# Experts' products from fp16 parts of both operands, the first layer's weights read in place

## The reference

```python
normed = _layernorm(hidden_states, rn_g, rn_b)
logits = (jnp.einsum('bld,ed->ble', normed, router_w) + router_b).astype(jnp.float32)
top_w, top_idx = jax.lax.top_k(logits, K)
...
for e in range(E):
    h = _layernorm(hidden_states, ln_g[e], ln_b[e])
    h = jax.nn.gelu(jnp.einsum('bld,di->bli', h, w1[e]) + b1[e], approximate=False)
    h = jnp.einsum('bli,id->bld', h, w2[e]) + b2[e]
    out = out + combine[..., e:e + 1] * h
```

## Time and profile before

| | us |
|---|---|
| median of 3 runs (lowest to highest) | 3234.09 (3232.27 to 3234.14) |
| span of the profiled execution | 3232.2 |
| attention, window 240 to 2460: PE busy | 2179.22 of 2220 |
| the same: DVE busy | 2213.41 of 2220 |
| experts, window 2700 to 3190: PE busy | 490.00 of 490 |
| experts, same: DVE, ACT, POOL busy | 194.25, 151.98, 247.68 |

### The profile page before, as it was taken

The page is one execution under the profiler, slowest core; times in us unless marked ns, Lnnn a source line. Parts: engine busy times, 40 slices in busy tenths (PEclk is TensorE's granted clock), DMA queues, the critical chain, the costliest instruction groups (busy, mean ns, idle before and its releaser), DMA issues. The chain is left out here.

```text
span 3232.2 us, 72457 instructions
## 1 busy us (share of the span) xinstructions
PE 3089.3 (96%) x29281; PEld 1389.4 (43%) x29282; DVE 2735.8 (85%) x2902; ACT 2502.6 (77%) x4689; POOL 453.2 (14%) x654
## 2 busy tenths in 40 slices
PE   8999999999999999999999999999999969999995
PEld 4333333333333333333333333333332658999995
DVE  3599999999999999999999999999998683433443
ACT  3269999999999999999999999999999552333333
POOL 2000000000000000000000000000000464555554
PEclk9989999999999999999999999999999979999997
DMA  6520101111020101011010101021002561222224
GB/s 159 124 45 15 35 21 30 30 34 28 15 35 24 28 15 35 29 30 28 28 28 18 34 21 28 15 51 28 15 9 83 206 227 34 38 38 36 36 37 124
DMA packets 101213, 152.92 MB, mean 47 GB/s; under 512 B 21592, under 2 KB 64464, under 8 KB 99248
## 3 DMA queue, kind: packets, MB, share of 16 engines
q1 hardware_dynamic: 85008, 130.03, 16.2%
q0 software_dynamic: 15904, 18.66, 3.6%
HBM read 88.35 MB, written 60.29 MB: 46 GB/s over the span
## 5 line engine op out<-in xcount | busy, mean ns | idle before, releaser
L1005 DVE TENSOR_REDUCE half_max<-scores 128x2 f32<-128x1024 f32 x2016 | 2297.4, 1219 | 10.5 <-PE scores L759 4.8
L930 ACT ACTIVATE probs<-bank 128x512 f32<-128x512 f32 x4012 | 2142.3, 595 | 142.5 <-PE bank L772 45.5
L831 PE MATMUL bank<-probs,V 128*32 128x256 f32 x16384 | 1309.6, 391 | 44.2 <-ACT probs L930 42.4
L759 PE MATMUL scores<-K,Q 48*128 48x512 f16 x4032 | 793.9, 388 | 3.0 <-SPq L542 2.2
L772 PE MATMUL bank<-Q,K 50*128 50x512 f16 x4012 | 789.7, 380 | 0.0
L831 PEld LDWEIGHTS bank<-probs,V 128*32 128x32 f32 x16384 | 322.5, 108 | 583.2 <-issue 517.7
L759 PEld LDWEIGHTS scores<-K,Q 48*128 48x128 f16 x4032 | 194.2, 93 | 834.6 <-DVE half_max L1005 532.2
L772 PEld LDWEIGHTS bank<-Q,K 50*128 50x128 f16 x4012 | 371.2, 94 | 183.0 <-ACT probs L930 4.2
L660 POOL TENSOR_SCALAR max_parts<-row_max 128x16 f16<-128x16 f32 x64 | 16.2, 253 | 2066.3 <-DVE row_max L1011 2066.3
L1604 ACT ACTIVATE h<-u 128x1024 f32<-128x1024 f32 x71 | 75.0, 1057 | 260.8 <-DVE u L1648 260.8
L1565 PE MATMUL pre<-xgT,w 128*128 128x128 f32 x2272 | 265.3, 275 | 2.3 <-ACT xgT L1598 2.3
(11 more groups left out here) (195 smaller groups left out, 1204.8 us busy)
## 6 DMA issues: line engine op xcount, KB each, us to landing
attended<-att SPq DMA_DIRECT2D x64, 256.0 KB, 2.5
W<-in_L_ffn_w_dram SPq DMA_DIRECT2D x16, 1024.0 KB, 6.4
Q<-q_parts SPq DMA_DIRECT2D x96, 128.0 KB, 6.6
K<-k_parts SPq DMA_DIRECT2D x96, 128.0 KB, 6.9
values<-attended SPq DMA_DIRECT2D x6, 2048.0 KB, 9.2
q_parts<-parts SPq DMA_DIRECT2D x64, 128.0 KB, 2.4
k_parts<-parts SPq DMA_DIRECT2D x64, 128.0 KB, 2.4
xT<-in_x_cols_dram SPq DMA_DIRECT2D x8, 512.0 KB, 4.9
```

Source lines behind the costliest of these rows:

```text
L759: mm = nc.tensor.matmul(scores[:, b, h, :], Q[p][r, c, up, t * P:(t + 1) * P], K[p][r, up, kc * TC:(kc + 1) * TC], start=True, stop=True)
L831: mm = nc.tensor.matmul(banks[att_bank[s // KB]][32 * u:32 * u + 32, q], V[wp][:, wk, u // 2, :], probs[:, 4 * s % RING + u, q], start=(wk ...
L930: nc.scalar.activation(probs[:, i % RING, :], banks[tile_bank[i]][:], ACT.Exp, scale=SCALE).then_inc(exp_done, 1)
L1005: nc.vector.tensor_reduce(half_max[lc % 2][:, :, up, t, kc], scores[:, b], AX.X, ALU.max).then_inc(max_done[b], 1)
```

## The change

Every float32 product of the experts' layers becomes three fp16 products. A float32 operand a is written as high + low, where high is a in fp16, and low is the rest in fp16; high x high, high x low and low x high are added up in PSUM. Weights are first multiplied by 2 to the 10th and activations by 2 to the 3rd, and the biases' additions take the factor out again (`UNLIFT`).

- The weights are split in the attention, by POOL (`split_w`): three instructions of 128 x 1024 for each of 4 units per pair, 32 units in all. SP loads each unit (`load_w`, 512 KB) and stores the two parts of w1 to DRAM (`store_w1`, `w1d`, 16 stores of 512 KB). The parts of w2 stay in `W2`, whose size in bytes is as before. The routing stage loads `W1` from `w1d`, as many bytes as before. POOL also clears the semaphores of the first stage that are no longer used.
- `take_w1` goes. `times_w1` reads `W1` in place: PE's sequencer loads the owner a second time per tile, and the weight operand has a register offset. 16 float32 matmuls become 48 fp16 matmuls of 128 columns.
- The second layer's 8 float32 matmuls become 24 fp16 matmuls of 256 columns, 16 with the high part of `h`, and then, behind a wait of their own, 8 with the low part.
- DVE splits the scaled rows (`high_x`, `low_x`, 128 x 256 each) and makes the low part of h (`low_h`, 128 x 1024). ACT makes its high part (`hs`). The order of the steps on ACT and DVE is changed with it.

```diff
+LIFT_W = 10
+LIFT_X = 3
...
+    w1d = nc.dram_tensor("w1_parts", (E, P, 2, KD, I), F16, kind="Internal").ap()
...
-        W2 = top.enter_context(nc.sbuf_tensor("W2", [P, E, IC, D], F32))
+        W2 = top.enter_context(nc.sbuf_tensor("W2", [P, E, 2, IC, D], F16))
...
-        W1 = top.enter_context(nc.sbuf_tensor("W1", [P, E, KD, I], F32))
+        W1 = top.enter_context(nc.sbuf_tensor("W1", [P, E, 2, KD, I], F16))
...
@@ -581,6 +590,23 @@
                 sp.dma_start(x1d[0:NT * P].rearrange("(p n j) d -> n p j d", p=P, n=QUADS)[q], x1[q % 2]
                              ).then_inc(x1_stored[q % 2], 16)
 
+            UNITS_W = 2 * KD
+
+            def load_w(it, m):
+                if it * UNITS_W + m >= 2:
+                    sp.wait_ge(w_split, it * UNITS_W + m - 1)
+                if m < KD:
+                    src = w1.rearrange("e (k p) i -> e k p i", p=P)[it, m]
+                    sp.dma_start(w_in[m % 2][:].rearrange("p j d -> p (j d)"), src).then_inc(w_loaded[m % 2], 16)
+                else:
+                    cs = slice((m - KD) * TPC, (m - KD + 1) * TPC)
+                    sp.dma_start(w_in[m % 2][:], w2.rearrange("e (c p) d -> e p c d", p=P)[it][:, cs]
+                                 ).then_inc(w_loaded[m % 2], 16)
+
+            def store_w1(it, m):
+                sp.wait_ge(w_split, it * UNITS_W + m + 1)
+                sp.dma_start(w1d[it][:, :, m, :], w_out[:]).then_inc(w1_stored, 16)
+
             load_max(1, 0)
             sp.dma_start(bet[:], beta.rearrange("(o d) -> o d", o=1).to_broadcast((P, D))).then_inc(bet_loaded, 16)
@@ -594,6 +620,10 @@
                 for lc in range(RC):
                     if lc > 0:
                         store_att(lc - 1)
+                    if lc < UNITS_W:
+                        load_w(it, lc)
+                    if 1 <= lc <= KD:
+                        store_w1(it, lc - 1)
                     if lc == CH and it < PAIRS - 1:
                         load_qk(0, it * 2 + 2)
                     if lc == 2:
@@ -609,9 +639,6 @@
                             sp.wait_ge(att_stored[p], 16 * HALFWAY * CH + 1)
                         load_heads(0)
                         load_heads(1)
-                    if lc == CH + 2:
-                        sp.dma_start(W2[:, bass.ds(it, 1)].rearrange("p o c d -> p (o c) d"),
-                                     w2.rearrange("e (c p) d -> e p c d", p=P)[it]).then_inc(w2_loaded, 16)
                     if it * RC + lc + 1 < CHUNKS:
                         load_max(it * RC + lc + 2, lc + 1)
...
@@ -666,7 +693,27 @@
                 nc.gpsimd.tensor_tensor(max_parts[:, 1, :], neg_max[:], max_parts[:, 0, :], ALU.subtract
                                         ).then_inc(max_parts_ready, 1)
 
+            def split_w(it, m):
+
+                unit = it * 2 * KD + m
+                whole = w_in[m % 2][:].rearrange("p j d -> p (j d)")
+                if m < KD:
+                    high, low = w_out[:, 0], w_out[:, 1]
+                else:
+                    cs = slice((m - KD) * TPC, (m - KD + 1) * TPC)
+                    high, low = (W2[:, it, i, cs, :].rearrange("p c d -> p (c d)") for i in range(2))
+                pool.wait_ge(w_loaded[m % 2], 16 * (unit // 2 + 1))
+                nc.gpsimd.tensor_scalar(whole, whole, 2.0 ** LIFT_W, None, ALU.mult).then_inc(w_lifted, 1)
+                pool.wait_ge(w_lifted, unit + 1)
+                if m < KD and it * KD + m > 0:
+                    pool.wait_ge(w1_stored, 16 * (it * KD + m))
+                nc.gpsimd.tensor_copy(high, whole).then_inc(w_high, 1)
+                pool.wait_ge(w_high, unit + 1)
+                nc.gpsimd.tensor_tensor(low, whole, high, ALU.subtract).then_inc(w_split, 1)
+
             cut_maxima(1, True)
+            for s in a["retired_sems"]:
+                pool.sem_clear(s)
             for it in range(PAIRS):
                 for lc in range(RC):
@@ -678,6 +725,8 @@
                             copy_v(0, it * 2 + 2)
                     if it * RC + lc + 1 < CHUNKS:
                         cut_maxima(it * RC + lc + 2)
+                    if lc < 2 * KD:
+                        split_w(it, lc)
                     if lc == CH:
                         if it == 0:
...
@@ -1269,7 +1320,7 @@
             sp.dma_start(rows[E * KD:LR], ln_b.rearrange("e (k d) -> (e k) d", d=P)).then_inc(rows_loaded, 16)
             sp.dma_start(rows[LR:LR + BR], b1.rearrange("e (c d) -> (e c) d", d=P)).then_inc(rows_loaded, 16)
             for e in range(E):
-                sp.dma_start(W1[:, e], w1[e].rearrange("(k p) i -> p k i", p=P)).then_inc(w1_loaded, 16)
+                sp.dma_start(W1[:, e], w1d[e]).then_inc(w1_loaded, 16)
             sp.dma_start(b2s[:].rearrange("p e d -> p (e d)"),
                          b2.rearrange("(o e) d -> o (e d)", o=1).to_broadcast((P, E * D))).then_inc(b2_loaded, 16)
...
-        w1 = [sb(f"w1_{i}", [P, KD, I], F32) for i in range(2)]
+        xs = [sb(f"xs{i}", [P, 2, D], F16) for i in range(2)]
         u = sb("u", [P, IC, P], F32)
-        h = [sb(f"h{i}", [P, IC, P], F32) for i in range(2)]
...
+
+        PRODUCTS = ((0, 0), (0, 1), (1, 0))
 
         def owner(eng, tile):
             return eng.value_load(owner_i[0:1, bass.ds(tile, 1)], min_val=0, max_val=E - 1)
@@ -1558,12 +1613,14 @@
                 mm.then_inc(turned, 1)
 
             def times_w1(n, p):
-                pe.wait_ge(w1_ready, n + 1)
-                pe.wait_ge(xgT_ready, KD * (n + 1))
+                e = owner(pe, n)
+                pe.wait_ge(xs_ready, 2 * (n + 1))
                 for c in range(IC):
                     for k in range(KD):
-                        mm = nc.tensor.matmul(pre[p][:, c, :], w1[p][:, k, c * P:(c + 1) * P],
-                                              xgT[p][:, k * P:(k + 1) * P], start=(k == 0), stop=(k == KD - 1))
+                        for i, (ws, s) in enumerate(PRODUCTS):
+                            mm = nc.tensor.matmul(pre[p][:, c, :], W1[:, bass.ds(e, 1), ws, k, c * P:(c + 1) * P].rearrange("p o i -> p (o i)"),
+                                                  xs[p][:, s, k * P:(k + 1) * P],
+                                                  start=(k == 0 and i == 0), stop=(k == KD - 1 and i == 2))
                 mm.then_inc(pre_ready, 1)
 
             def step(n, it, q, left):
@@ -1575,11 +1632,16 @@
                 if left >= 2:
                     turn_rows(n + 2, it + (q % XB + 2) // XB, (q + 2) % XB)
                 e = owner(pe, n)
-                pe.wait_ge(h_ready, n + 1)
+                pe.wait_ge(high_ready, n + 1)
                 pe.wait_ge(y_ready, n + 1)
                 for c in range(IC):
-                    mm = nc.tensor.matmul(py[p][:, 0:D], h[p][:, c, :],
-                                          W2[:, bass.ds(e, 1), c, :], start=(c == 0), stop=(c == IC - 1))
+                    for ws in range(2):
+                        nc.tensor.matmul(py[p][:, 0:D], hs[p][:, 0, c, :], W2[:, bass.ds(e, 1), ws, c, :],
+                                         start=(c == 0 and ws == 0), stop=False)
+                pe.wait_ge(low_ready, n + 1)
+                for c in range(IC):
+                    mm = nc.tensor.matmul(py[p][:, 0:D], hs[p][:, 1, c, :], W2[:, bass.ds(e, 1), 0, c, :],
+                                          start=False, stop=(c == IC - 1))
                 mm.then_inc(py_ready, 1)
 
...
@@ -1601,7 +1665,13 @@
 
             def gelu(n, p):
                 act.wait_ge(u_ready, n + 1)
-                nc.scalar.activation(h[p][:], u[:], ACT.Gelu).then_inc(h_ready, 1)
+                if not isinstance(n, int) or n >= 1:
+                    act.wait_ge(low_ready, n)
+                nc.scalar.activation(h[:], u[:], ACT.Gelu).then_inc(h_ready, 1)
+                if not isinstance(n, int) or n >= 2:
+                    act.wait_ge(py_ready, n - 1)
+                act.wait_ge(h_ready, n + 1)
+                nc.scalar.mul(hs[p][:, 0], h[:], 2.0 ** LIFT_X).then_inc(high_ready, 1)
 
             def weigh(n, it, q):
                 act.wait_ge(part_loaded[q % XB], 16 * (it + 1))
@@ -1612,10 +1682,10 @@
 
             def step(n, it, q, left):
                 p = q % 2
+                if left >= 2:
+                    norm_rows(n + 2, p)
                 if left >= 1:
                     gelu(n + 1, 1 - p)
-                if left >= 2:
-                    norm_rows(n + 2, p)
                 weigh(n, it, q)
 
             norm_rows(0, 0)
@@ -1633,36 +1703,51 @@
 
         @block.vector
         def _(dve):
-            def take_w1(n, p, used):
+            def add_b1(n, p):
                 e = owner(dve, n)
-                if used is not None:
-                    dve.wait_ge(pre_ready, used)
-                nc.vector.tensor_copy(w1[p][:], W1[:, bass.ds(e, 1), :, :].rearrange("p o k i -> p (o k) i")
-                                      ).then_inc(w1_ready, 1)
-
-            def add_b1(n, p, used):
-                e = owner(dve, n)
```

(48 more changed lines are left out.)

38 lines of the change are left out of this document (25 added, 13 removed).

## The result

| | before | after |
|---|---|---|
| median (lowest to highest) of 4 runs each | 3233.18 (3232.18 to 3234.14) | 3320.09 (3318.77 to 3321.21) |
| span of the profiled execution | 3232.2 | 3319.4 |
| mean granted clock | 0.98 | 0.98 |

The ratio is 1.0268, 95% interval 1.0253 to 1.0282. Slower was forecast, but the loss is 87 us and not 20, and the time lies above the range's end of 3298.

What follows compares the result with a forecast made beforehand. PE's sequencer was to replace the array as bound: 1.50 + 1.98 + 3.68 + 0.15 + 0.21 = 7.52 us a tile against 7.24, so 0.28 x 70 = +20 us on 3234.09, 3254 us; range 3228 to 3298.

Steps and rivals of the forecast that it cites:

- a share of the loop's branch: PE's sequencer, per tile: with a semaphore instruction and wait values, priced as two more instructions, 0.21 us.
- 16 more in the first layer and 16 in the second: PE's sequencer: 32 register instructions per tile with one matmul each, at 115 ns (106 to 124), 3.68 us.
- the 5.66 of the sum: PE's sequencer, per tile: all register instructions, 1.98 us for 16 preceding two matmuls plus 3.68 us for 32 preceding one.
- the small terms: PE's sequencer, per tile: 0.15 us for 24 instructions without a register, 0.21 us for semaphore, waits and branch share.
- 1.50 for two owners: PE's sequencer, per tile: the owner's load done twice at 0.75 us each.
- The array: PE's array in the experts: 56 to 60 ns per first-layer matmul with its load, 5.5 to 5.7 us a tile.
- the rival of the weight loads: Experts: loads overlap matmuls only in part, array needs 6.9 us a tile; 3208 us if issue is hidden; chance 0.04.
- that of the hidden issue: Experts: register instructions overlap with the array, which sets 5.5 us a tile; 3112 us, chance 0.05; smaller gain 0.04.
- The other engines: Experts: the work of DVE (3.1 to 3.8 us), ACT (3.5) and POOL per tile hides below 7.5 us.
- The clock: Experts: PE's granted clock stays at 1.00, with matmuls filling 5.5 of 7.5 us.
- The forecast's rival of the clock: Experts: clock falls to 1.2 GHz, array needs 10.7 us for one tile in three; 3330 us, chance 0.09.
- The attention: Splitting the weights on POOL there costs nothing; the attention ends within 3 us of where it did.

Runs made afterwards that it cites:

- e1: The kernel after with the experts' loop written out and nothing else changed: 3274.1 us.
- e11: The kernel after with PE's loop as 12 iterations of 4 tiles instead of 6 of 8, other engines' loops unchanged: 3286.36 us.
- e5: The kernel after without the first layer's third product (low part of the weights by high part of x): 3141.47 us.
- e6: e1 with the owner's register kept from a tile's first layer for its second, so PE loads the owner once: 3214.97 us.
- e4: The kernel after with DVE copying the first-layer weights' parts to a fixed address, and the loop written out: 3200.46 us.
- e8: e4 with DVE's copy of the weights moved ahead of its addition of b1, all three products kept: 3164.52 us.
- e2: The kernel after with DVE copying the first-layer weights' parts to a fixed address, loop kept: 3216.65 us.
- e9: e2 with nine one-column matmuls added per tile, 1519 instructions in PE's loop: 3221.3 us in its one run.
- e10: Projections and attention of the kernel after, with the weight split, and routing and experts of the kernel before: 3232.97 us.

## Why the prediction was right or wrong

The sign was right, for the stated reason: the array got faster and PE's sequencer became the bound. The size was wrong. The time between the first and the last transposes divides by the runs: 503.1 us before, 544.2 in e1, 555.3 in e11, 587.2 after.

| part | forecast | measured |
|---|---|---|
| 70 steps by the sequencer's pace | +20 | +41 (e1 - before) |
| upkeep of a loop whose body is short, eleven branches | within 0.21 us a tile | +11 (e11 - e1) |
| the long body's branches back | nothing | +32 (after - e11) |
| ahead of and behind the tiles | 0 | +3 |

**The step that failed: "a semaphore instruction, wait values and a share of the loop's branch: two more instructions of about 0.1 us, 0.21".** I took the branch's price from a body of 959 instructions and asked only what an instruction more costs in the sequencer, not what a body of 1647 does to the branch. Some 32 us lie there, half of the 67 that I missed, and rather 35, since e11 has six branches more, at 0.5 us each. Each long branch stops PE for 3.5 to 3.6 us and again for 1.2 to 1.5 us, and the body is fetched anew. Another 11 us are the upkeep of a loop with a short body, which my 0.21 was meant to cover. With a short body the same change gives 3286, inside the range.

**"16 more in the first layer and 16 in the second, each with only one matmul and its load ... I take the middle, 115".** Mis-sized. The trace shows 127 to 133 ns whether one matmul follows or two (and e5 128 for both). The bounds went only up to the measured 124; the mean is higher, as about one step in ten takes 150 to 300 ns. 48 x 131 ns are 6.3 us against the 5.66 of the sum, 44 us over 70 tiles. What the small terms added (0.15 and 0.21, 25 us) doesn't show beside it in written-out tiles, so that the tiles came out only 21 us over the forecast: two errors in part made up for each other. 6.3 + 1.50 for two owners give 7.8; e1's tiles are 7.77. One owner's load was worth 0.83 by e6, by instructions 0.75.

**The array**, 56 ns for a first-layer matmul with its load: right (e4, e8). A tile of e8 in which nothing is late took 5.73 us, where the array's estimate was 5.5 to 5.7. So the rival of the weight loads was rightly small, and so was that of the hidden issue.

**The other engines**: right. `u`, GELU, the parts of h and x take 1.22, 1.06, 1.22 and 0.43 us and hide; DVE and ACT wait for PE.

**The clock**: "stays at 1.00" was wrong in part. Windows of the kernel after, across the branch's stall and the first layer after it, and across a common first layer:

```profile
2817.50:2821.00 3.50, 0.00 (x0) 0.00 (x0) 1.56 (x2) 0.51 (x1) 1.37 (x1) 0.79 0.04 9
2823.30:2827.10 3.80, 3.80 (x43) 3.69 (x42) 0.00 (x0) 0.00 (x0) 0.50 (x1) 0.60 0.12 34
2995.70:2999.80 4.10, 4.10 (x48) 3.24 (x49) 1.56 (x2) 0.51 (x1) 0.76 (x1) 1.00 0.00 0
```

The granted clock falls to 0.50 (1.2 GHz) after each of the five long branches, PE having stood still, and is back at 1.00 within that tile or the next. It is a result of the stall: in e2, e5, e9 and e11, whose branches are short, it stays at 1.00 from 2700 us to the last tile. It also stood at 0.50 in the stage's first tiles (windows 2683.0:2686.4 and 2689.8:2693.2 of the kernel after), ahead of the loop; e1 and e11 have such stretches too. It costs little by itself. In the chain above, the 43 matmuls behind the stall take 4.02 / 43 = 93 ns each, and the 48 of the first layer before it 4.07 / 48 = 85. Over the five passes the 43 take 3.96 to 4.78 us where 85 ns each would be 3.66: 3.5 us in all. The forecast's rival of the clock (3330 us) came close to the time by chance; its mechanism, one tile in three at 10.7 us, isn't there.

**The attention**: "ends within 3 us" holds (e10).

What stays open: in the kernel after, loop tiles without a branch take 8.1 us and in e11 7.83 to 7.95. Blocks of code arrive during the former, but they arrive as often in e1, whose tiles take 7.8, so their arrival alone doesn't explain it, and no run parted the cause. Nor did a run part the 11 us of the short loop's upkeep, or say why the limit lies where it does.

## What to carry to other kernels

- When matmuls get cheaper, recount what PE's sequencer does per tile: here a register address costs about 0.13 us and a loaded register 0.8, hidden under float32 matmuls and fully paid under fp16 ones. A copy to a fixed address by an engine with room, issued early enough, bought 2.1% where reading in place lost 1.3%, both written out.
- Count a loop body's instructions on each engine before and after a change that multiplies them, and look at the branch back in the trace; a body of half the length can be had by a loop of its own for that engine.
- A step's small terms should be priced at the new size of the thing, not the old one.

## What the runs showed of the hardware

- A branch back of PE takes 0.21 to 0.25 us with a body of up to 1519 instructions, and 3.3 to 3.8 us with 1647 or 1663, with a second gap of 1.2 to 1.5 us in the first layer behind it in the kernel after. No run had a length between 1519 and 1647, and no branch took a time between.
- A body of 1647 instructions is fetched again in every pass (9 packets of 16 KB in one), one of 826 not at all.
- A step with a register address takes the sequencer 128 ns on average with one fp16 matmul and its load behind it, and as much with two (e5).
- fp16 matmuls of 128 columns with a weight load each follow each other every 56 ns over 48 in a row (e4, e8).
